# First graph layer of a two-layer GNN: own rows of the first far unit by one-hot matmuls, centring and residual sum on GpSimd

## What is computed

```
edge_index = jnp.stack([src, dst])
h = jnp.maximum(_layernorm(x, axis=-1), 0.0)
x = x + _L0_gnn_ref(h, edge_index, W0, b0, W1, b1, W2, b2)
h = jnp.maximum(_layernorm(x, axis=-1), 0.0)
x = x + _L1_gnn_ref(h, W1, b1, W2, b2, gamma, beta, src, dst)

# layer 0, an MLP on every edge, summed at row
row, col = (edge_idx[0], edge_idx[1])
h = jnp.concatenate([x[row], x[col]], axis=-1)     # 128 wide
h = jax.nn.softplus(h @ W0 + b0)                   # 128
h = jax.nn.softplus(h @ W1 + b1)                   # 128
h = h @ W2 + b2                                    # 64
return jax.ops.segment_sum(h, row, num_segments=x.shape[0])

# layer 1
z = h + jax.ops.segment_sum(h[src], dst, num_segments=n)
z = jnp.maximum(z @ W1 + b1, 0.0) @ W2 + b2
z = relu(batch_norm(z) * gamma + beta); z = h + z
```

## Time and profile before

| | us |
|---|---|
| median of 3 runs | 2696.3 |
| lowest, highest | 2668.45, 2700.9 |
| the profiled execution | 2709.65 |
| its span in the profile | 2708.0 |
| mean granted TensorE clock | 0.822 of full |
| `edges0`, from the first index copy to the last | 302.3 to 1800.0 |

### The profile page before, as it was taken

The page is one execution under the profiler, slowest core; times in us unless marked ns, Lnnn a source line. Parts: engine busy times, 40 slices in busy tenths (PEclk is TensorE's granted clock), DMA queues, the critical chain, the costliest instruction groups (busy, mean ns, idle before and its releaser), DMA issues. The chain is left out here.

```text
span 2708.0 us, 37399 instructions
## 1 busy us (share of the span) xinstructions
PE 1645.4 (61%) x9524; PEld 1173.3 (43%) x9524; DVE 1475.0 (54%) x4143; ACT 977.4 (36%) x2307; POOL 1200.3 (44%) x1151
## 2 busy tenths in 40 slices
PE   0111277777777777777777777775354555645556
PEld 0111155555555655555555655554232323323334
DVE  6999556655555556555566555655233433333334
ACT  0566444444444444444444444442011111111134
POOL 0899633434333333433334433332655655655610
PEclk9999988888888878888898878887677777777775
DMA  1334213222222223222232222232222222222229
GB/s 38 111 121 125 78 43 75 60 56 58 57 56 56 64 67 61 59 58 57 64 72 58 59 56 56 56 69 56 41 51 44 50 48 44 50 45 47 50 79 307
DMA packets 345722, 183.07 MB, mean 68 GB/s; under 512 B 283916, under 2 KB 309913, under 8 KB 345671
## 3 DMA queue, kind: packets, MB, share of 16 engines
q1 hardware_dynamic: 292388, 119.46, 17.5%
q0 software_dynamic: 32928, 37.40, 8.5%
q10 hardware_dynamic: 20354, 25.65, 2.6%
HBM read 126.61 MB, written 55.79 MB: 67 GB/s over the span
## 5 line engine op out<-in xcount | busy, mean ns | idle before, releaser
L770 POOL DMA_INDIRECT fast_gathered<-h_table,fast_gather_i x588 | 569.5, 969 | 954.8 <-DVE fast_gather_i L784 787.2
L1120 POOL DMA_INDIRECT fast_gathered<-h_neighbours_table,fast_index_i x441 | 422.3, 958 | 344.8 <-issue 221.2
L791 DVE TENSOR_SCALAR fast_e<-fast_e 128x384 f32<-128x384 f32 (+1 forms) x490 | 194.9, 400 | 658.0 <-ACT fast_e L1028 582.3
L1028 ACT ACTIVATE fast_e<-bank,b_s 128x384 f32<-128x384 f32 (+1 forms) x490 | 295.2, 621 | 566.2 <-remote 306.3
L799 DVE SCALAR_TENSOR_TENSOR fast_h<-bank,b_s,fast_e 128x384 f32<-128x384 f32 (+1 forms) x490 | 303.5, 659 | 0.6 <-ACT fast_e L1035 0.6
L959 PE MATMUL bank<-fast_h,w_s 128*128 128x384 f32 (+1 forms) x490 | 275.0, 649 | 1.9 <-DVE fast_h L799 1.9
L1203 PE MATMUL bank<-fast_z_in,gw_s 128*128 128x512 f32 x98 | 92.4, 1043 | 289.3 <-ACT fast_z_in L1218 217.8
L1035 ACT ACTIVATE fast_e<-fast_e 128x384 f32<-128x384 f32 (+1 forms) x490 | 265.0, 560 | 6.9 <-issue 0.7
L945 PE MATMUL bank<-fast_in_t,w_s 128*128 128x384 f32 x294 | 163.8, 645 | 166.5 <-issue 86.4
L1218 ACT ACTIVATE fast_z_in<-node_sums 128x512 f32<-128x512 f32 x49 | 29.3, 597 | 635.2 <-DMA h_table<-prep_normed 589.8
L997 PE MATMUL node_sums<-fast_message,fast_hot 128*128 128x80 f32 x1568 | 227.5, 298 | 12.1 <-issue 12.1
(11 more groups left out here) (226 smaller groups left out, 3086.9 us busy)
## 6 DMA issues: line engine op xcount, KB each, us to landing
fast_local<-local_rows SPq DMA_DIRECT2D x49, 384.0 KB
h_neighbours_table<-fast_h_rows SPq DMA_DIRECT2D x49, 320.0 KB
fast_self_rows<-h_neighbours_table SPq DMA_DIRECT2D x49, 320.0 KB
h_table<-prep_normed ACTq DMA_DIRECT2D x49, 256.0 KB
fast_own_rows<-h_table SPq DMA_DIRECT2D x49, 256.0 KB
x_plus_h<-fast_x SPq DMA_DIRECT2D x49, 256.0 KB
finish_resid<-x_plus_h SPq DMA_DIRECT2D x49, 256.0 KB
prep_xin<-in_x SPq DMA_DIRECT2D x48, 256.0 KB
```

Source lines behind the costliest of these rows:

```text
L770: pool.indirect_dma_start(gathered[slot][:, at:at + D], None, h0_t, bass.IndirectOffsetOnAxis(ap=gather_i[q][:, n:n + 1], axis=0))\
L791: V.tensor_scalar(e[at][:, 0:w], e[at][:, 0:w], EXP_CLAMP, None, ALU.min).then_inc(done, 1)
L1028: A(e[at][:, 0:w], psum[:, 0:w], ACT.Exp, bias=b_s[:, :]).then_inc(done, 1)
L1120: pool.indirect_dma_start(gathered[q][:, c * MW:(c + 1) * MW], None, h1_t, bass.IndirectOffsetOnAxis(ap=index_i[q][:, c:c + 1], axis=0))\
```

## The change

`EXPANDED` becomes `(0, 1, 2)`: the first far unit too takes its own side from SBUF. `centre` and `add_h1` move from VectorE's list to GpSimd's, between and behind the gathers.

```diff
-        EXPANDED = (1, 2)
+        EXPANDED = (0, 1, 2)
...
                             return body
-                        rounds(pool, [(0, gather(k)) for k in range(GK)], BLOCKS, 2)
+
+                        def centre(b, q, turn):
+                            hold(pool, mean_done, b + 1, passed_pool)
+                            wait_from(pool, normed_done, b - 1, passed_pool)
+                            nc.gpsimd.tensor_tensor(groups(centred[q][:, :], D), groups(total[q][:, :], D),
+                                                    mean[q][:, :].unsqueeze(2).to_broadcast([128, SUBS, D]),
+                                                    ALU.subtract).then_inc(centred_done, 1)
+
+                        def add_h1(b, q, turn):
+                            hold(pool, normed_done, b + 1, passed_pool)
+                            wait_from(pool, x1_stored[q], 16 * turn, passed_pool)
+                            nc.gpsimd.tensor_tensor(groups(x1[q][:, :], D), groups(total[q][:, :], D),
+                                                    groups(h1_rows[q][:, :], MW)[:, :, 0:D], ALU.add).then_inc(x1_ready, 1)
+                        rounds(pool, [(0, gather(0)), (0, gather(1)), (LAG + 2, add_h1), (0, gather(2)),
+                                      (LAG + 1, centre)], BLOCKS, 2)
...
                         def sum_columns(b, q, turn):
                             dve.wait_ge(total_ready, b + 1)
+                            wait_from(dve, centred_done, b - 1)
...
-                        behind = [[(LAG + 2, variance)], [(LAG + 2, normalise)], [(LAG + 2, add_h1)],
-                                  [(LAG + 1, sum_columns)], [(LAG + 1, centre), (0, indices)]]
+                        behind = [[(LAG + 2, variance)], [(LAG + 2, normalise)], [], [(LAG + 1, sum_columns)],
+                                  [(0, indices)]]
```

More of the change, by code:

```diff
@@ L856, in mean_of_sum @@
                             V.tensor_scalar(mean[q][:, :], mean[q][:, :], 1.0 / D, None, ALU.mult).then_inc(mean_done, 1)
[L858 to L862, removed]
                         def variance(b, q, turn):
```

## The result

The changed kernel takes 2971.89 us (median of 4 runs, 2967.24 to 2980.32) where the kernel before takes 2695.03 us (median of four runs, one more than the three given above): a ratio of 1.1052, 95% interval 1.0974 to 1.113. The forecast was 2994 us in a range from 2850 to 3190. The profiled execution took 2974.7 us, 265 more than the one before (2709.65).

A forecast was written before the change was run, and what follows sets the result against it. Waits, not a full engine, bound the kernel; `edges0` took 31.55 us a block. Legs of 15.1 + 23.1 make 38.2, 6.65 more in 46 rounds (306 us), less about 8 and 13.35 to the median: 2994 us, range 2850 to 3190.

The forecast's parts named there:

- this is a closed ring, once a block: `edges0`: index copy, nine gathers, residual sum, centring, square, slots and next index copy wait for each other: 38.2 us a block.
- First leg: From index copy to ScalarE's square: 1.15 + 11.5 gathers + 2.1 elementwise + 0.4 gaps and hand-over, 15.1 us.
- other than 1.0 or 3.1 us: Sign that the prediction is wrong: elementwise instructions on GpSimd taking any time but these two.
- Second leg: From square to next index copy: first softplus, three gaps between pairs, a fourth, and the last piece, 23.1 us.
- VectorE loses two instructions ... the second leg counts them at nothing: VectorE in `edges0`: two instructions of 0.68 us leave, both ahead of idle time, so no gain counted.
- The clock: TensorE behind the new wait: lower clock taken for first to second pair; high clock would be 1.75 us less.
- The hold: ScalarE's unnamed wait in old slot 2, tied to the gathers: covered by the new wait, giving back some 6 us.
- Sum: `edges0` block 38.2 us in place of 31.55, 6.65 more in 46 rounds, 306 us; about 8 gained earlier.
- The first: Rival: old slot 2's stall stays as well, block 44.55 us, about 3286 us; chance 0.08.
- The third: Rival: GpSimd's two instructions take 3.12 us each, 4.2 us more a block, 3185 us; chance 0.08.
- The fourth: Rival: little change, with the shortest leg behind the square and a shorter one ahead of it; chance 0.05.
- The second: Rival: faster, three gathers less end the stall 3.8 us sooner in 48 blocks, 2514 us; chance 0.04.

The follow-up runs named there:

- e2: Changed kernel with `EXPANDED` taken back to (1, 2), so the move to GpSimd alone with twelve gathers: 3151.97 us, ratio 1.1468.
- e3: Changed kernel with only the centring moved, to the head of GpSimd's round ahead of the gathers: 2623.71 us, ratio 0.9534.
- e4: Changed kernel with the residual sum put back on VectorE, expansion and centring as changed: 2956.12 us in one run.
- e6: Kernel before with only its gathers spaced six, three and three: 2168.29 us, ratio 0.9963 beside a kernel before of 2177.07 us.
- e1: Kernel before with the expansion alone, centring and residual sum staying on VectorE: 2664.34 us, ratio 0.9675.
- e11: Kernel before with gathers spaced six, three and three, run again beside a kernel before of 2690.81 us: 2731.83 us, ratio 1.0174.
- e12: Same kernel as e5, run again beside a kernel before of 2690.81 us: 2451.28 us, ratio 0.9108.
- e5: Changed kernel with centring and residual sum ahead of gathers spaced three, three and three: 2276.24 us, ratio 1.0457 beside 2177.07 us.
- e8: Kernel before with the index copy moved from the end of slot 4 to the end of slot 1: 2186.64 us in one run.

## Why the prediction was right

*What decides.* The step "this is a closed ring, once a block" is shown: by the wait in the profile, by e2 (three gathers more, 3.4 us more) and by e3 (centring ahead of the gathers: faster than before).

*First leg.* Forecast 15.1 us, measured 14.5. Gathers 1.275 each as forecast. The centring took 1.05, the residual sum 1.27 where 1.04 was put; by the prediction's own sign ("other than 1.0 or 3.1 us") that price was wrong. Of the 0.4 us for gaps almost nothing was needed: centring and residual sum each start 0.02 us behind the gather ahead of them.

*Second leg.* Forecast 1.3 + 7.0 + 5.0 + 3.8 + 4.1 + 1.9 = 23.1, measured 1.3 + 6.54 + 5.11 + 4.75 + 4.04 + 1.32 = 23.06. The sum is right by luck: errors of -0.46, +0.95 and -0.58 us cancel. The 7.0 held 0.4 for the expansion's matmuls, which cost nothing there (e2 has the same 6.54 without them). The third to fourth pair takes 4.75 and not 3.8, though the clock is at its upper level there. The 3.83 that it was read from has ScalarE's unnamed wait right ahead of it; where none stands there, the slot takes 4.75 with the expansion (changed, e4) and without it (e2, e6), so the term was mis-sized and the expansion is not the reason. And the last piece is 1.32: "VectorE loses two instructions ... the second leg counts them at nothing" is wrong for the centring, which had stood between the last bias and the index copy; 0.6 us of the 1.9 were its own.

*The clock.* Taken as low for the slot behind the wait, and it is: 0.54 granted in the block shown and 0.50 to 0.51 in the corresponding stretches of three others (from 983, 1058 and 1095), while before it was low behind the stall in one of the two blocks shown.

*The hold.* "So the stall of the old slot 2 is covered": shown by the missing wait, and by e3, where it is back once the ring is gone.

*Sum.* 6.01 us a block in place of 6.65; the forecast of 298 us for the profiled execution was 33 too high, and 46 x 0.64 = 29 of these come from the block.

*The rivals.* The first would need a second stall behind the square: there is none. The third would need GpSimd at 3.12: all 49 centrings took 1.042 to 1.061. The fourth, little change, would need a short first leg, and it is 14.5. The second, the faster one, had its mechanism right and its price too high: the end of the hold did move by 4.0 us in e1, but the block gained 1.1. Its premise, that the hold alone sets the block, left out the work behind the hold and the clock that it runs at.

## What to carry to other kernels

Before an instruction is moved to an engine that looks idle, look at what stands ahead of it in that engine's queue, and what that in turn waits for: here a 1 us step was put behind 11.5 us of gathers which start only when the slots that wait for the step are done. Its place in the list was worth 15% of the kernel before (ratios 1.105 and 0.953), the choice of engine 1.5% (e3 against e1). If an engine in a trace waits long for another that is itself mostly idle, look for such a ring; one line of order opens it.

## What the runs showed of the hardware

*Runs of gathers hold up what waits for TensorE, in some runs.* Where the kernel before takes some 2700 us, ScalarE's unnamed wait ends 0.9 to 2.4 us behind the end of the last gather of a run: of twelve (before, 1.9 to 2.4 in 39 of 41 blocks), nine (e1, 1.7 to 2.1; and e3, with the residual sum inside the run, 0.9 to 1.1) or six (e11, 1.3 in the block shown). Groups of three with 1.5 to 1.9 us between them did not do it (e12). Where it takes 2177 us nothing of this is seen (e5 to e8). The end of the run is not the whole of it: in many blocks of before a shorter unnamed wait ends inside the run (24 in the loop, 71.6 us). One block of before shows both, and TensorE beside them:

```profile
1055.41 0.50 PE L934 MATMUL bank<-ident,fast_gathered 128*128 128x128 f32 x3
...
1060.82 0.91 PE L945 MATMUL bank<-fast_in_t,w_s 128*128 128x384 f32 x2 [3.61 <-issue]
...
1063.35 1.81 PE L977 MATMUL node_sums<-w_s,fast_h 128*128 128x64 f32 x8
```

```profile
1060.28 0.49 ACT L1020 ACTIVATE fast_in_t<-bank 128x384 f32<-128x384 f32 x1 [3.28 <-remote]
1066.67 1.16 ACT L1028 ACTIVATE fast_e<-bank,b_s 128x384 f32<-128x384 f32 x2 [5.91 <-remote]
```

ScalarE's copy (L1020) needs the three transposes, over by their records at 1055.91, and starts 4.4 us later, 4.2 us before the twelfth gather ends. Its `exp` (L1028) needs the matmuls of L945, over by their records at 1061.73, and starts 4.9 us later, while TensorE goes on with the matmuls that stand behind them in its queue. So in these records the matmuls themselves run on, and what comes late is the news of their end. The ends of matmuls are modelled in the profile, so this is a strong hint and no proof. Another one is how the landings of DMAs show in the DMA view. The profile gives a time to landing only if it finds all updates of a semaphore. For e5, which ran where no hold was seen:

```profile
fast_local<-local_rows SPq DMA_DIRECT2D x49, 576.0 KB, 5.2
```

and for e12, the same kernel where the kernel before has the hold:

```profile
fast_local<-local_rows SPq DMA_DIRECT2D x49, 576.0 KB
```

The time is missing, so updates are missing from that trace. It is no accident of this line: the trace of e5 holds 23,155 records of updates by DMAs, that of e12 13,921. A single line can still be whole beside a kernel before of 2744 us (e2, 4.4 us). A crowded path of semaphore updates would fit all of this; it is argued and not shown.

*GpSimd and VectorE exclude each other, in both directions.* In e12 VectorE's index copy, 0.17 us in the changed kernel, takes 1.92:

```profile
677.12 1.92 DVE L798 COPY fast_gather_i<-far_idx 128x18 int32 x1
```

GpSimd's centring (676.71 to 677.77) and residual sum (677.71 to 678.99) ran meanwhile in their usual times, and the copy ends at 679.04. In the preparation of the kernel before either engine pays, by who starts first: a centring that starts at 82.79, ahead of VectorE's instruction at 82.85, takes 1.04 and VectorE's 3.26; one that starts at 115.46, behind VectorE's at 115.26, takes 3.12 and VectorE's 2.41. This is what the Trainium skill (SBUF — State Buffer, Who interferes with whom) states of the port pair that the two engines share; the first to start keeps it. The traces agree for these and for e12's centring, which started ahead of the copy; the residual sum started behind the copy and went ahead of it all the same. So a tiny instruction can be held for two large ones beside it. Here it costs little: e12's gathers wait for TensorE and not for the copy (10.45 us in the block shown), and the first softplus pair comes 5.13 us behind the start of the copy, where it is 5.03 in e3, whose copy takes 0.17.

*GpSimd's elementwise price is not one number*: 1.27 us for the residual sum, an addition of two full tiles of 128x512, and 1.05 us for the centring, a subtraction in which one operand is a broadcast of 128x8. The residual sum also reads one tile in steps, 64 of every 80 columns; which of these makes the difference no run separates.
